# Blocks of uneven size, dense features copied to a row of their own, and a later third layer in a DLRM tower on one Trainium2 core

## The reference

```python
e = jnp.stack([tbl_0[ids[:, 0]], ..., tbl_25[ids[:, 25]]], axis=1)      # 2048 x 26 x 128
combined = jnp.concatenate([dense_features[:, None, :], e], axis=1)     # 2048 x 27 x 128
interactions = jnp.einsum('bfd,bgd->bfg', combined, combined)
z = jnp.concatenate([dense_features, interactions[:, iu, ju]], axis=1)  # upper triangle: 351
h = jnp.concatenate([z, r_dense_features], axis=1)                      # 2048 x 607
h = jnp.maximum(h @ W_top1 + b_top1, 0.0)                               # 512
h = jnp.maximum(h @ W_top2 + b_top2, 0.0)                               # 256
y = h @ W_top3                                                          # 1
```

## Time and profile before

| | us |
|---|---|
| median of 3 runs | 428.47 (428.03 to 428.75) |
| the profiled execution | 426.81 |
| its span, first to last instruction | 425.0 |
| TensorE busy (matmuls) | 382.4, 90% |
| GpSimd busy | 258.2, 61% |
| VectorE busy | 224.4, 53% |
| ACT busy | 145.3, 34% |
| mean granted TensorE clock | 0.956 of full speed |

### The profile page before, as it was taken

One profiled execution on the slowest core, in us unless ns is written; L12 is line 12 of the kernel. 1 busy time (PEld: TensorE's weight loads), 2 busy tenths in 40 slices (PEclk: granted clock), 3 DMA queues, 4 the chain that ended last, 5 costly groups with the idle time before them and its releaser, 6 DMA issues.

```text
span 425.0 us, 7915 instructions
## 1 busy us (share of the span) xinstructions
PE 382.4 (90%) x3308; PEld 274.1 (64%) x3308; DVE 224.4 (53%) x414; ACT 145.3 (34%) x320; POOL 258.2 (61%) x248
## 2 busy tenths in 40 slices
PE   6758977359999979999999979999999979999997
PEld 6646865248466648889456638889456638889442
DVE  1847995005944439807925349807925349807300
ACT  2342643212322234443223234443223234442421
POOL 6788887750777777731777777721777777720000
PEclk9886989859999999999999989999999989999999
DMA  7992232210122132320222232410232232310000
GB/s 196 388 326 73 63 78 59 68 51 10 45 70 67 49 82 63 105 52 12 57 68 61 60 76 58 106 45 17 55 70 57 59 78 60 77 28 4 2 0 0
DMA packets 19872, 30.74 MB, mean 72 GB/s; under 512 B 5657, under 2 KB 13977, under 8 KB 19836
## 3 DMA queue, kind: packets, MB, share of 16 engines
q0 software_dynamic: 7680, 15.74, 14.3%
q1 hardware_dynamic: 12148, 14.48, 12.1%
q10 hardware_dynamic: 8, 0.01, 0.0%
HBM read 30.21 MB, written 0.01 MB: 71 GB/s over the span
## 4 chain that ended last, share of the span: by engine, by line
PE 76%; POOL 16%; issue 5%; ACT 2%; DMA 1%; POOLq 0%
PE mix_ps L420 17%; POOL rows L340 16%; PE emb_ps L363 14%; PE emb_ps L364 14%; PE mix_ps L393 7%; PE emb_ps L393 7%; PE mix_ps L431 6%; PE emb_ps L374 6%; PE mix_ps L439 3%; PE emb_ps L405 1%; ACT h L508 1%; ACT emb L469 1%; DMA rows<-table,gather_ids 1%; DMA gather_ids<-ids_gathered 0%; ACT emb L459 0%
## 5 line engine op out<-in xcount | busy, mean ns | idle before, releaser
L340 POOL DMA_INDIRECT rows<-table,gather_ids x240 | 257.2, 1072 | 116.3 <-issue 70.4
L536 DVE TENSOR_SCALAR hot<-lids,row_number 128x512 fp32r<-128x512 int16 x352 | 160.2, 506 | 92.0 <-PE emb_ps L364 83.6
L363 PE MATMUL emb_ps<-hot,table_hl 128*128 128x512 f32 x352 | 154.5, 439 | 10.8 <-DVE hot L536 10.8
L364 PE MATMUL emb_ps<-hot,table_hl 128*128 128x512 f32 x352 | 140.8, 400 | 0.0
L363 PEld LDWEIGHTS emb_ps<-hot,table_hl 128*128 128x128 f32 x352 | 68.3, 194 | 30.6 <-issue 13.7
L364 PEld LDWEIGHTS emb_ps<-hot,table_hl 128*128 128x128 f32 x352 | 68.4, 194 | 19.1 <-issue 6.3
L469 ACT ACTIVATE emb<-emb_ps 128x512 f32<-128x512 f32 x64 | 43.2, 689 | 103.0 <-PE emb_ps L374 101.8
L459 ACT ACTIVATE emb<-emb_ps 128x512 f32<-128x512 f32 x44 | 50.2, 1140 | 81.7 <-PE emb_ps L364 81.7
L546 DVE STREAM_TRANSPOSE turned<-mix_ps 32x832 uint32<-32x832 uint32 (+1 forms) x24 | 25.2, 1049 | 58.6 <-PE mix_ps L393 58.2
L374 PE MATMUL emb_ps<-ident,rows 128*128 128x128 f32 x256 | 39.9, 284 | 16.4 <-DMA rows<-table,gather_ids 16.4
L374 PEld LDWEIGHTS emb_ps<-ident,rows 128*128 128x128 f32 x256 | 31.8, 146 | 29.8 <-DMA rows<-table,gather_ids 18.7
(11 more groups left out here) (27 smaller groups left out, 106.0 us busy)
## 6 DMA issues: line engine op xcount, KB each, us to landing
lids<-ids_looked_up SPq DMA_DIRECT2D x44, 128.0 KB, 3.1
raw<-table SPq DMA_DIRECT2D x11, 512.0 KB, 10.5
rows<-table,gather_ids POOLq DMA_INDIRECT x240, 2.6
rows<-dense SPq DMA_DIRECT2D x16, 64.0 KB, 1.8
w_sb<-w_pairs SPq DMA_DIRECT2D x2, 256.0 KB
w_sb<-w SPq DMA_DIRECT2D x1, 512.0 KB
w_sb<-w_dense SPq DMA_DIRECT2D x1, 256.0 KB
w_stage<-w_dense SPq DMA_DIRECT2D x1, 256.0 KB
```

What stands on the lines that cost most here:

```text
L340: pool.indirect_dma_start(out=rows[:, use % ROW_SLOTS, q, :], out_offset=None, in_=tables[GATHERED[g]], in_offset=bass.IndirectOffsetOnAxi ...
L363: pe.matmul(bank[:, :], table_hl[:, i, 0, cols], hot[:, n % HOTS, :], start=(c == 0), stop=False)
L364: pe.matmul(bank[:, :], table_hl[:, i, 1, cols], hot[:, n % HOTS, :], start=False, stop=(c == CHUNKS - 1)).then_inc(hot_used, 1)
L536: dve.tensor_scalar(hot[:, n % HOTS, :], lids[:, k % LIDS, :], row_number[:, c:c + 1], None, ALU.is_equal).then_inc(hot_ready, 1)
```

## The change

- Blocks have 2, 4, 4, 4 and 2 tiles (256, 512, 512, 512, 256 samples) and look up 11, 11, 11, 10 and 8 tables on TensorE; the rest is gathered: 166 lookups of a tile and 250 gathers, where there were 176 and 240. A group has still up to four features; with 16 gathered tables and dense a tile has five groups in place of four, with 18 and dense too.
- Codes, lookups, layers and copies are as wide as their block; a narrow block stands in the middle of `emb`.
- GpSimd no longer waits for the grams of the block before.
- ACT copies each tile's dense features from PSUM to `dense_x` (L485), and `l1` with c = 3 reads them there.
- The third layer is planned 9 us later (`L3_LATER`), the weight sum at 36 in place of 58.
- The planned times follow from each block's size. `rows` has 7 slots in place of 8, `hot` 9 in place of 10, which makes room for `dense_x`.

```diff
-BLOCK_LOOKUPS = [11] * 4
+BLOCK_TILES = [2, 4, 4, 4, 2]
+BLOCK_LOOKUPS = [11, 11, 11, 10, 8]
...
-    ROW_SLOTS = 8
+    ROW_SLOTS = 7
...
-    HOTS = 10
+    HOTS = 9
...
-    FIRST, LENGTH, GROUP_TIME = 98.0, 94.0, 5.0
+    LENGTH = [2.9 + 5.5 * 4 * n + 3.7 * n for n in BLOCK_TILES[:1]]
+    for b in range(1, BLOCKS):
+        LENGTH.append(5.1 * BLOCK_TILES[b - 1] + (0.93 * BLOCK_LOOKUPS[b] + 5.7) * BLOCK_TILES[b])
+
+    L3_LATER = 9.0
...
-        at(after + 27.0, "l3", b)
-    at(58, "weights")
...
+        at(after + 8.0 + 17.5 * part + L3_LATER, "l3", b)
+    at(36, "weights")
...
+        dense_x = sb("dense_x", [128, BLOCK])
...
-                if t % IN_BLOCK == 0:
-
-                    wait(pool, grams_done, t - 1)
...
-                    x = dense_part
+                    x = dense_x[:, 0:WIDE[b]]
...
-                    wait(act, dense_used, t // IN_BLOCK)
...
+                    wait(act, dense_used, BLOCK_OF[t])
+                    act.activation(by_turn(dense_x[:, PLACE[t] * TILE:PLACE[t] * TILE + TILE]),
+                                   by_number(bank[:, 128 * n - 128:128 * n]), ACT.Copy)
```

More of the change, by code:

```diff
@@ L53, in dlrm_tower @@
     TILES = BATCH // TILE
-    BLOCKS = BATCH // BLOCK
-    IN_BLOCK = BLOCK // TILE
+    BLOCKS = len(BLOCK_TILES)
+    FIRST_TILE = [sum(BLOCK_TILES[:b]) for b in range(BLOCKS + 1)]
+    BLOCK_OF = [b for b in range(BLOCKS) for _ in range(BLOCK_TILES[b])]
+    PLACE = [t - FIRST_TILE[BLOCK_OF[t]] for t in range(TILES)]
+    WIDE = [TILE * n for n in BLOCK_TILES]
+    assert len(BLOCK_OF) == TILES and all(n % 2 == 0 for n in BLOCK_TILES)
+    SECOND, PAIR_WIDE = 32, 59
+    EMB_AT = [(BLOCK - wide) // 2 * PAIR_WIDE for wide in WIDE]
     def grouped(features):
@@ L121, in dlrm_tower @@
     for b in range(BLOCKS):
[L122 to L135, removed]
+        rows_at, first = last_rows(b), FIRST_TILE[b]
+        for j in range(BLOCK_TILES[b]):
+            t = first + j
+            at(rows_at - 3.0 if j == 0 else rows_at + 0.5 + 3.6 * (j - 1), "gram", t)
+            at(rows_at + 0.4 if j == 0 else rows_at + 0.5 + 3.6 * j + 0.1, "turn", t)
+            at(rows_at + 0.5 + 3.6 * (j + 1) + 0.2, "pairs", t)
         after = ends(b)
@@ L278, in wait_emb_bank, with by_turn, by_number, samples @@
                 engine.wait_ge(emb_placed, placed[before])
-        dense_part = bass.AP(emb, FEATURES - 1, [[EMB_WIDE, 128], [32 * PAIR_WIDE, BLOCK // 64], [SECOND, 2], [PAIR_WIDE, 32]])
+        def by_turn(x):
+            return x.rearrange("p (g e q) -> p g q e", g=2, e=2)
+        def by_number(x):
+            return x.rearrange("p (g q e) -> p g q e", g=2, e=2)
+        def samples(b):
+            return slice(FIRST_TILE[b] * TILE, FIRST_TILE[b + 1] * TILE)
         @block.sync
@@ L362, in look @@
                     cols = slice(DIM * c, DIM * c + DIM)
[L363 to L364 removed]
+                    pe.matmul(bank, table_hl[:, i, 0, cols], hot[:, n % HOTS, 0:WIDE[b]], start=(c == 0), stop=False)
+                    pe.matmul(bank, table_hl[:, i, 1, cols], hot[:, n % HOTS, 0:WIDE[b]],
                               start=False, stop=(c == CHUNKS - 1)).then_inc(hot_used, 1)
@@ L438, in l3 @@
                 for m in range(N2):
-                    last = pe.matmul(layer_bank(2)[0:1, :], w3_sb[:, m:m + 1], h2[:, m, :], start=(m == 0), stop=(m == N2 - 1))
+                    last = pe.matmul(layer_bank(2, WIDE[b])[0:1, :], w3_sb[:, m:m + 1], h2[:, m, 0:WIDE[b]], start=(m == 0), stop=(m == N2 - 1))
                 last.then_inc(l3_full, 1)
@@ L496, in z @@
                 act.wait_ge(z_full, 3 * b + c + 1)
-                act.activation(z_x[0:KCH[c], c, :], emb_bank(("z", b, c))[0:KCH[c], :], ACT.Copy).then_inc(z_ready, 1)
+                act.activation(z_x[0:KCH[c], c, 0:WIDE[b]], emb_bank(("z", b, c), WIDE[b])[0:KCH[c], :], ACT.Copy).then_inc(z_ready, 1)
             def h1(b, n):
```

101 lines of the change are left out of this document (52 added, 49 removed).

## The result

| | before | after |
|---|---|---|
| median of 4 runs each, us | 428.25 | 408.15 |
| lowest to highest, us | 427.85 to 428.75 | 407.08 to 410.28 |
| profiled execution, its span, us | 426.81, 425.0 | 407.08, 405.3 |

The ratio is 0.9536, with a 95% interval of 0.949 to 0.9582: 20 us faster. The forecast was 397 us in a range of 388 to 411. The sign and the range hold; the centre is 11 us too low, and it is worth knowing where those 11 us lie.

What follows compares the result with a forecast made beforehand. Gathers were taken to bound the kernel to about 92 us, then TensorE. Last grams at 69.1, 147.1, 235.6, 320.9 and 374.2 plus a 19.6 tail gave span 393.8, scaled to 397 us; range 388 to 411.

Steps and rivals of the forecast that it cites:

- Dense copy, -3.7: First layer on TensorE: reading dense features from a contiguous row takes 3.5 us for 7.21, 3.7 less per 512 samples.
- the rival that the stride isn't the cause: First layer: the dense part stays at 7.21 us from dense_x, +15 us, 412; chance 0.05.
- Third layer, -4.0: Third layer planned 9 us later: TensorE's 2.4 us stop and the low clock's 1.6 go, -4.0 a block.
- Lost cover, +0.4 for 512 samples: Behind a block's last gram: the shorter dense part no longer hides all of VectorE's turn and new codes; 0.3 to 0.4 open.
- Gathers: GpSimd without its wait for grams: 1.33 us a gather; the edit gives nothing by itself but keeps the others' gain.
- Seven slots, not eight, still let POOL run 26 gathers, 35 us, ahead: Gathered rows: GpSimd keeps enough lead with one slot fewer, so rows come in time for blocks 1 to 4.
- 256-wide lookups: Lookup matmuls on TensorE in 256-sample blocks: 0.123 us each, 1.97 a table.
- the rival that weight loads show: 256-wide matmuls take 0.164 us for 0.123, 5.3 us in block 4, 402; at the far bound 417; chance 0.09.
- Block 0: First block, 256 samples: 64 codes at 0.26 us, low halves and weight sum take 25.2 from 33.2; second gram ends at 69.1.
- codes over 0.30: Sign of a wrong forecast: 256-wide codes on VectorE taking over 0.30 us, where 0.26 was taken.
- The sum of blocks 1 to 3: TensorE's time between the ends of last grams: 78.0 us for block 1, 88.5 for block 2, 85.3 for block 3.
- Tail: Behind the last gram: 19.6 us against 30.6, with TensorE standing 3 us and 1.5 added for low clock.

Runs made afterwards that it cites:

- b_dense: The kernel before with only the dense features copied to a row of their own and seven row slots for eight: 543.26 us against 560.7, ratio 0.9667.

## Why the prediction was right, and 11 us short

**Dense copy, -3.7: right.** 3.70 us with its first start-up, 605 ns an instruction; the rival that the stride isn't the cause is refuted, since the same instructions take 1066 ns as soon as they read at the stride again. The copies cost ACT 0.42 instead of 0.3.

**Third layer, -4.0: right** for the second and third block of before, behind whose stops the clock had fallen; behind the first block's it had not, and there only the stop of 2.2 could go. The kernels with the old time show that only the stop is certain; that before lost the clock twice on its chip is a fact of its trace that the sum could use, not a rule.

**Lost cover, +0.4 for 512 samples: right,** within 0.2: the next lookup begins 3.97 us after the dense part does, forecast 3.85.

**Gathers: right on the pace,** 0.99 us busy and 0.30 between two, so 1.29 against 1.33, and right that the edit gives nothing alone. The forecast expected no waits for rows behind block 0 and there is one, of 2.14 us in block 3. The step that failed is "Seven slots, not eight, still let POOL run 26 gathers, 35 us, ahead": it counts 15 gathers in four groups. In block 3 a tile has 16 in five groups, and seven slots hold 22: GpSimd stood for 11.18 us when it had issued 22 of that block's gathers, and for 7.5 more in four waits up to 281.15, and that time was lacking at its end. The wait of TensorE is most of the 2.9 of block 3.

**256-wide lookups: right.** In block 4 they are 0.12 us apart, forecast 0.123; the rival that weight loads show, at 0.164, is refuted. The rule on overlap that the prediction takes from the Trainium skill ("TensorE: Matmul & The Clock Gate") stands there in the section "The mechanism"; these rows speak against it as the 512-wide ones did.

```profile
359.86 0.28 PE L380 MATMUL emb_ps<-hot,table_hl 128*128 128x256 f32 x1
359.98 0.28 PE L381 MATMUL emb_ps<-hot,table_hl 128*128 128x256 f32 x1
```

**Block 0, the term that was mis-sized most.** "I take 0.26" for a 256-wide code. Alone that is what it takes from start to start. Beside gathers it takes 0.31, and in block 0 gathers run all the time. From 33.77 to 62.58 the codes, low halves and weight sum take 28.8 us where 25.2 were forecast: 3.3 more for 64 codes and 0.3 for the rest. The ids came 0.6 later. Together that is 4.1 of the 4.3. The bounds, 0.20 and 0.40, held it; the value was drawn from the code's width alone, out of the 0.406 of a 512-wide code. Beside those codes too gathers were running, and there it was the gather that was held up:

```profile
37.26 1.28 POOL L340 DMA_INDIRECT rows<-table,gather_ids  x1 [0.30 <-issue]
```

In block 0 of the changed kernel it is the other way round: from 3 to 64 us all gathers but four take 0.94 or 0.95, and none over 1.29. But the width doesn't decide who pays. Later in the kernel before single 512-wide codes are held up as well: 40 of the 352 take over 0.6, undisturbed ones 0.47 to 0.49. One of them stands beside the gather of 206.45, which took its usual 0.94:

```profile
206.92 0.72 DVE L536 TENSOR_SCALAR hot<-lids,row_number 128x512 fp32r<-128x512 int16 x1
```

So a term for VectorE beside gathers, some 0.2 us for a gather, was missing from the sum, which had priced the contention on GpSimd alone (1.71 beside low halves). Which of the two waits when stays open. The prediction named codes over 0.30 as the sign of an error, and that is the one that came.

**A term that was missing: 0.2 to 1.4 us a block.** The sum of blocks 1 to 3 was made from a whole block of before, and in that one TensorE didn't stop before the first gram; before the second it stopped for 0.85. There twelve transposes (1.47 from 185.47) lay behind the last lookup. In block 1 it has only four (0.60 from 134.75), and ACT's copy of it takes 1.10 from 134.94: 0.76 us of stop at the first gram, and 1.07 at the second, for the copy of the last group. Together 1.0 more, of the 1.7 of block 1. In block 2 no transpose at all is left between the last lookup and the gram:

```profile
224.51 0.39 PE L381 MATMUL emb_ps<-hot,table_hl 128*128 128x512 f32 x1
226.09 3.94 PE L410 MATMUL mix_ps<-emb 128*64 128x52 f32 x128 [1.20 <-ACT emb L476]
```

With 1.07 at the second gram that is 1.4 more, and with 0.1 at the first lookup all of the 1.5 of block 2. In block 3 this copy lies inside the wait for rows, and the second gram's stop adds 0.2. Block 4 had 1.35 us for copies in its sum and stopped for 0.73 and 1.07, and for 0.40 once more for ACT's relu (L522): 0.85 of its 1.3. That the stop at the first gram is the copy of the last lookup was shown by the earlier lookups, with which block 4's is gone. Some 0.6 us of block 1 and 0.4 each of blocks 3 and 4 I can't place.

**Tail: right** (19.37 for 19.6), with the clock at 0.91 and a stop of 2.74 us, as forecast 3.

## What to carry to other kernels

When an edit shortens an engine's work, list what used to lie under that work at every boundary: here the stops behind ACT's copies grew by 0.2 to 1.4 us a block, some 3 us in all. Removing a wait on an engine with time to spare gives nothing, yet putting one in front of a queue that is nearly the bound costs its whole lead: 60 gathers at 1.36 us made a block of 99 us out of one of 80. And size an operation from a row that has the same neighbours at work, not only the same shape.

## What the runs showed of the hardware that was not expected

- Gathers issued by GpSimd slow VectorE's comparisons (128x256, int16 to fp32r): eight take 2.18 us without and 2.64 with them, and the low halves hardly (1.22 and 1.27). In block 0 of the changed kernel the gathers beside them keep their 0.94; beside 512-wide ones either can be held up, the gather to 1.28, or one code from 0.48 to 0.72. The Trainium skill ("SBUF — State Buffer", "SBUF: two separate sides") describes the port that the two share as an exclusive lock that the one that comes first holds for its whole instruction; of VectorE's instructions only those in a two-port mode take it, or, against a GpSimd one that reads SBUF, those with two inputs in SBUF. That each can wait for the other agrees. That VectorE loses only some 0.2 us for each gather of 0.94 does not, if a gather is one instruction; in which mode the comparisons run no run shows.
- On three of the chips each gather within the small matmuls of the grams cost TensorE 1.4 us, with instruction durations unchanged. On the ordinary ones it cost nothing: 17.03 us for four grams with 14 gathers beside them, 17.0 with none.
- The clock drop behind a stop of 2.2 us isn't certain: the third layer takes 3.49 and 3.53 us in two blocks of before and 1.88 in another, and 1.88 behind all three such stops of `b_dense` (2.21) and of the changed kernel with the third layer at its old time (1.74 to 1.89).
